# Two transformer layers on eight cores: order of the expert weight loads, and second k and v buffers in the WKV loop

## The reference

```python
x = x + _layernorm(_L0_attn_ref(_layernorm(x), ...))   # phase A: causal attention, 16 heads
x = x + _layernorm(_L0_ffn_ref(_layernorm(x), ...))    # phase B: attention, then a mixture of 8 experts
x = x + _layernorm(_L1_attn_ref(_layernorm(x), ...))   # phase C: the WKV recurrence
x = x + _layernorm(_L1_ffn_ref(_layernorm(x), ...))    # phase D: feed-forward with per-token LoRA
```

```python
for e in range(E):                       # E = 8, FFN = 2048, HID = 1024
    w1 = w13[e, :FFN]; w3 = w13[e, FFN:]
    g = silu(h @ w1.T) * (h @ w3.T)
    out = out + einsum('tf,hf->th', g, w2[e]) * wfull[:, e:e + 1]
```

```python
k = xk @ W_k.T; v = xv @ W_v.T; r = sigmoid(xr @ W_r.T)
new_p = max(p, u + k_t); so = exp(max(p - new_p, -30)); sc = exp(max(u + k_t - new_p, -30))
wkv_t = (so * q + sc * v_t) / (so + sc + 1e-9)
p, q = the same kind of update with the decay w
y = r * wkv;  out = y @ W_o.T
```

## Time and profile before

| | us |
|---|---|
| runs shown | 8763.72, 8841.24, 8338.84 |
| their median | 8763.72 |
| the profiled execution | 8342.41 |
| its span on core 3, the slowest core | 8340.7 |
| spans of the eight cores | 8273.8 to 8340.7 |
| PE busy on core 3 | 5667.9 (68%) |
| DVE busy | 2138.5 (26%) |
| ACT busy | 1978.9 (24%) |
| POOL busy | 170.9 (2%) |

### The profile page before, as it was taken

The page is one execution under the profiler, slowest core; times in us unless marked ns, Lnnn a source line. Parts: engine busy times, 40 slices in busy tenths (PEclk is TensorE's granted clock), DMA queues, the critical chain, the costliest instruction groups (busy, mean ns, idle before and its releaser), DMA issues.

```text
span 8340.7 us, 77939 instructions; the slowest of 8 cores (8273.8 to 8340.7 us)
## 1 busy us (share of the span) xinstructions
PE 5667.9 (68%) x21912; PEld 2164.4 (26%) x21912; DVE 2138.5 (26%) x3361; ACT 1978.9 (24%) x3520; POOL 170.9 (2%) x206
## 2 busy tenths in 40 slices
PE   5777764355887378889898989898821332537992
PEld 1222221021222133334343434343300111102330
DVE  3101112333111412222222222222237334230113
ACT  1256652214664110101010101001110232212111
POOL 0000000000000000000000000000000111000000
PEclk7656667665666689989899999999955666768995
DMA  2000002210000041332323231413120000221203
GB/s 61 11 1 1 1 12 61 60 21 1 1 1 11 1 82 34 68 61 51 59 54 61 41 71 31 81 33 69 36 84 23 12 12 18 62 61 26 56 2 79
DMA packets 82929, 313.97 MB, mean 38 GB/s; under 512 B 10136, under 2 KB 10520, under 8 KB 63032
## 3 DMA queue, kind: packets, MB, share of 16 engines
q0 software_dynamic: 26112, 207.99, 13.0%
q1 hardware_dynamic: 56416, 101.00, 4.5%
HBM read 483.31 MB, written 33.62 MB: 62 GB/s over the span
## 4 chain that ended last, share of the span: by engine, by line
PE 61%; DVE 12%; DMA 12%; ACT 8%; issue 6%; SPq 1%; POOL 1%; DVEq 0%; ACTq 0%; POOLq 0%
PE B_pso L1031 11%; PE B_psg L992 11%; PE B_psg L999 11%; DMA B_w3s<-b_w3T 3%; PE D_psi L1469 3%; PE D_pso L1487 3%; PE A_pmm L292 3%; PE A_pss L360 2%; PE C_pmm L1167 2%; PE B_pav L789 2%; PE A_pav L388 2%; ACT B_E L119 2%; ACT A_E L119 2%; PE B_pss L762 2%; DVE C_A L119 1%
## 5 line engine op out<-in xcount | busy, mean ns | idle before, releaser
L992 PE MATMUL B_psg<-B_H,B_w1s 128*128 128x512 bf16 x4096 | 980.7, 383 | 325.4 <-DMA B_w3s<-b_w3T 310.4
L999 PE MATMUL B_psg<-B_H,B_w3s 128*128 128x512 bf16 x4096 | 972.8, 381 | 0.0
L1031 PE MATMUL B_pso<-B_gall,B_w2b 128*128 128x512 bf16 x4096 | 902.9, 383 | 2.3 <-issue 0.5
L119 ACT ACTIVATE B_gsil<-B_psg 128x512 f32<-128x512 f32 x512 | 305.7, 597 | 2161.1 <-PE B_psg L992 2161.0
L119 DVE TENSOR_TENSOR B_gall<-B_gsil,B_psg 128x512 bf16<-128x512 f32 x512 | 351.9, 687 | 1759.0 <-PE B_psg L999 1759.0
L992 PEld LDWEIGHTS B_psg<-B_H,B_w1s 128*128 128x128 bf16 x4096 | 402.2, 98 | 819.8 <-issue 346.0
L1031 PEld LDWEIGHTS B_pso<-B_gall,B_w2b 128*128 128x128 bf16 x4096 | 401.7, 99 | 513.1 <-issue 45.1
L999 PEld LDWEIGHTS B_psg<-B_H,B_w3s 128*128 128x128 bf16 x4096 | 402.6, 98 | 489.5 <-issue 13.6
L1167 PE MATMUL C_pmm<-C_xk,C_wk 128*128 128x512 bf16 x256 | 72.7, 455 | 497.8 <-DVE C_Y L119 346.0
L119 ACT ACTIVATE B_E<-B_pss 128x512 bf16<-128x512 f32 (+3 forms) x640 | 341.2, 533 | 192.3 <-PE B_pss L762 135.2
L757 PE MATMUL B_pss<-B_qT,B_kT 32*128 32x512 bf16 (+3 forms) x640 | 284.4, 490 | 129.3 <-issue 108.2
(11 more groups left out here) (308 smaller groups left out, 4879.0 us busy)
## 6 DMA issues: line engine op xcount, KB each, us to landing
B_w1s<-b_w1T POOLq DMA_DIRECT2D x64, 1024.0 KB, 8.6
B_w3s<-b_w3T POOLq DMA_DIRECT2D x64, 1024.0 KB, 13.2
B_w2b<-b_w2T POOLq DMA_DIRECT2D x8, 4096.0 KB, 25.4
A_xc<-xin SPq DMA_DIRECT2D x32, 256.0 KB, 3.8
A_xr<-xin SPq DMA_DIRECT2D x32, 256.0 KB, 4.2
xm<-A_ost SPq DMA_DIRECT2D x32, 256.0 KB, 3.3
B_xc<-xm SPq DMA_DIRECT2D x32, 256.0 KB, 3.3
BT_xr<-xm SPq DMA_DIRECT2D x32, 256.0 KB, 3.2
```

The source lines that it names most:

```text
L119: instr = real(*a, **kw)
L992: mm = t.matmul(ps_g1[:], w1s[sb][:, dt * CH + fs * 128: dt * CH + (fs + 1) * 128], H[:, dt * T + c * CH:dt * T + (c + 1) * CH], start=(dt ...
L999: mm = t.matmul(ps_g3[:], w3s[sb][:, dt * CH + fs * 128: dt * CH + (fs + 1) * 128], H[:, dt * T + c * CH:dt * T + (c + 1) * CH], start=(dt ...
L1031: mm = t.matmul(ps_o[pb][:], w2b[:, ft * 1024 + ot * 128: ft * 1024 + (ot + 1) * 128], g_all[:, ft * 1024 + ch * CH: ft * 1024 + (ch + 1) ...
```

## The change

In phase B the tiles of the experts are allocated once for all experts, and the guards (`slab_guard`, `g1_free`, `evac` and the others) are no longer reset. In each expert the loads of slabs 0 and 1 are issued first, each pair guarded by the last matmul that read its buffer pair; the load of w2 is issued after them, guarded by `b_done` and by a new token `w2_users`, the last matmul that read `w2b`. In the loop over the slabs these first two pairs are taken from `pre_toks` and not loaded again in half 0.

In phase C `kb_` and `vb_` become two buffers each, used in turn. `A2` is no longer a tile; its contents are written over `pst`. The PSUM banks are freed by ACT's evacuations alone. Three tokens keep the order of the other tiles: `kv_consumed[idx]` (`y_tok` of two passes ago) ahead of the evacuations of k and v, `prev_y` ahead of those of r, and `prev_y` with `prev_ecv` ahead of Exp(k).

```diff
+        slab_guard = [None, None]
...
+        w2_users = None
+        bar9 = ctx.bar()
         for e in range(NEXP):
...
+                pre_toks = {}
+                for slab in range(2):
+                    sb = slab % 2
+                    pre_toks[(1, slab)] = load_wcast(
+                        ctx, W["w1T"][e * 128:(e + 1) * 128, slab * 4096:(slab + 1) * 4096],
+                        w1s[sb][:], f"qs1{sb}",
+                        pre=[slab_guard[sb]] + (bar9 if e == 0 else []))
+                    pre_toks[(3, slab)] = load_wcast(
...
                 w2tok = [load_wcast(ctx, W["w2T"][e * 128:(e + 1) * 128, :], w2b[:], "qw2B",
-                                    pre=[b_done] + (bar9 if e == 0 else []))]
-                slab_guard = [None, None]
...
+                                    pre=[b_done, w2_users] + (bar9 if e == 0 else []))]
...
+                        if (1, slab) in pre_toks:
+                            t1 = pre_toks.pop((1, slab))
+                            t3 = pre_toks.pop((3, slab))
+                        else:
...
                             b_done = pt
+                            w2_users = pt
...
-                kb_ = S3("C_kd", [128, T], F32)
-                vb_ = S3("C_vd", [128, T], F32)
+                kbufs = [S3("C_kd0", [128, T], F32), S3("C_kd1", [128, T], F32)]
+                vbufs = [S3("C_vd0", [128, T], F32), S3("C_vd1", [128, T], F32)]
...
-                            ctx.waits(s, [pt])
                             if dstb is not None:
+                                ctx.waits(s, [pt, kv_consumed[idx]])
...
                             else:
+                                ctx.waits(s, [pt, prev_y])
...
-                    ctx.waits(s, kv_tok)
+                    ctx.waits(s, kv_tok + [prev_y, prev_ecv])
...
+                    A2 = pst[:, 0:T]
...
-                    evac[0] = y_tok
-                    evac[1] = y_tok
+                    kv_consumed[idx] = y_tok
+                    prev_y = y_tok
```

More of the change, by code:

```diff
@@ L943, in phase_l0ffn @@
         esM.close()
+        esA = contextlib.ExitStack()
+        SA = lambda n, sh, dt: esA.enter_context(nc.sbuf_tensor(n, sh, dt))
+        PA = lambda n, sh: esA.enter_context(nc.psum_tensor(n, sh, F32))
+        g_all = SA("B_gall", [128, NTT * 1024], BF16)
+        w1s = [SA("B_w1s0", [128, NDT * CH], BF16), SA("B_w1s1", [128, NDT * CH], BF16)]
+        w3s = [SA("B_w3s0", [128, NDT * CH], BF16), SA("B_w3s1", [128, NDT * CH], BF16)]
+        _gs = SA("B_gsil0", [128, CH], F32)
+        gsil = [_gs, _gs]
+        w2b = SA("B_w2b", [128, NTT * 1024], BF16)
+        wf_row = SA("B_wfrow", [1, CH], F32)
+        wb_sb = SA("B_wb", [128, CH], F32)
+        ps_g1 = PA("B_psg1", [128, CH])
+        ps_g3 = PA("B_psg3", [128, CH])
+        ps_o = [PA("B_pso0", [128, CH]), PA("B_pso1", [128, CH])]
+        ps_wb = PA("B_pswb", [128, CH])
+        tmpo = gsil[0]
         wf_guard = [None]
@@ L947, in phase_l0ffn @@
         b_done = None
-        for e in range(NEXP):
[L949 to L965, removed]
-                w2tok = [load_wcast(ctx, W["w2T"][e * 128:(e + 1) * 128, :], w2b[:], "qw2B",
-                                    pre=[b_done] + (bar9 if e == 0 else []))]
-                slab_guard = [None, None]
[L970 to L974, removed]
@@ new lines, in phase_l0ffn @@
+        slab_guard = [None, None]
+        gs_tok = [None, None]
+        g1_free = None
+        g3_free = None
+        evac = {}
+        wb_free = None
+        w2_users = None
+        bar9 = ctx.bar()
+        for e in range(NEXP):
+            if True:
+                pre_toks = {}
[6 more added lines that the diff above has]
+                    pre_toks[(3, slab)] = load_wcast(
+                        ctx, W["w3T"][e * 128:(e + 1) * 128, slab * 4096:(slab + 1) * 4096],
+                        w3s[sb][:], f"qs3{sb}",
+                        pre=[slab_guard[sb]] + (bar9 if e == 0 else []))
+                w2tok = [load_wcast(ctx, W["w2T"][e * 128:(e + 1) * 128, :], w2b[:], "qw2B",
+                                    pre=[b_done, w2_users] + (bar9 if e == 0 else []))]
@@ L977, in phase_l0ffn @@
                         sb = slab % 2
[L978 to L985, removed]
+                        if (1, slab) in pre_toks:
+                            t1 = pre_toks.pop((1, slab))
+                            t3 = pre_toks.pop((3, slab))
+                        else:
+                            t1 = load_wcast(
+                                ctx, W["w1T"][e * 128:(e + 1) * 128, slab * 4096:(slab + 1) * 4096],
+                                w1s[sb][:], f"qs1{sb}", pre=[slab_guard[sb]])
+                            t3 = load_wcast(
+                                ctx, W["w3T"][e * 128:(e + 1) * 128, slab * 4096:(slab + 1) * 4096],
+                                w3s[sb][:], f"qs3{sb}", pre=[slab_guard[sb]])
                         for fs in range(4):
@@ L1045, in phase_l0ffn @@
         moe_tok = [radd]
+        esA.close()
         esH2.close()
@@ L1147, in phase_l1attn @@
                 A1 = S3("C_A1", [128, T], F32)
-                A2 = S3("C_A2", [128, T], F32)
                 rbuf = S3("C_rd", [128, T], BF16)
@@ L1152, in phase_l1attn @@
                 y_tok = None
+                prev_y = None
+                prev_ecv = None
+                kv_consumed = [None, None]
                 evac = {}
@@ L1155, in phase_l1attn @@
                 for dt in range(NDT):
+                    idx = dt % 2
+                    kb_ = kbufs[idx]
+                    vb_ = vbufs[idx]
                     wtok = []
@@ L1196, in phase_l1attn @@
                                            op0=ALU.add, op1=ALU.max)
-                    v.tensor_tensor(out=A2[:], in0=pst[:, 0:T], in1=A1[:], op=ALU.subtract)
-                    tv = v.tensor_scalar(out=A2[:], in0=A2[:], scalar1=-30.0, scalar2=None, op0=ALU.max)
+                    A2 = pst[:, 0:T]
+                    v.tensor_tensor(out=A2, in0=pst[:, 0:T], in1=A1[:], op=ALU.subtract)
+                    tv = v.tensor_scalar(out=A2, in0=A2, scalar1=-30.0, scalar2=None, op0=ALU.max)
                     ctx.waits(s, [tv])
-                    eo_tok = s.activation(out=A2[:], in_=A2[:], func=AF.Exp)
+                    eo_tok = s.activation(out=A2, in_=A2, func=AF.Exp)
                     v.scalar_tensor_tensor(out=ekv[:], in0=kb_[:], scalar=u_sc, in1=A1[:],
@@ L1207, in phase_l1attn @@
                     ctx.waits(v, [ec_tok, em_tok])
-                    tv = v.scalar_tensor_tensor(out=A2[:], in0=A2[:], scalar=EPS9, in1=ekv[:],
+                    tv = v.scalar_tensor_tensor(out=A2, in0=A2, scalar=EPS9, in1=ekv[:],
                                                 op0=ALU.add, op1=ALU.add)
@@ L1211, in phase_l1attn @@
                     ecv_tok = g.tensor_tensor(out=ekv[:], in0=ekv[:], in1=vb_[:], op=ALU.mult)
+                    prev_ecv = ecv_tok
                     ctx.waits(s, [tv])
-                    s.activation(out=A2[:], in_=A2[:], func=AF.Ln)
-                    rcp = s.activation(out=A2[:], in_=A2[:], func=AF.Exp, scale=-1.0)
+                    s.activation(out=A2, in_=A2, func=AF.Ln)
+                    rcp = s.activation(out=A2, in_=A2, func=AF.Exp, scale=-1.0)
                     ctx.waits(v, [rcp])
@@ L1218, in phase_l1attn @@
                     v.tensor_tensor(out=A1[:], in0=A1[:], in1=ekv[:], op=ALU.add)
-                    v.tensor_tensor(out=A1[:], in0=A1[:], in1=A2[:], op=ALU.mult)
+                    v.tensor_tensor(out=A1[:], in0=A1[:], in1=A2, op=ALU.mult)
                     y_tok = v.tensor_tensor(out=Ybf[:, dt * T:(dt + 1) * T], in0=A1[:],
                                             in1=rbuf[:], op=ALU.mult)
-                    evac[0] = y_tok
-                    evac[1] = y_tok
+                    kv_consumed[idx] = y_tok
+                    prev_y = y_tok
                 y_last = [y_tok]
```

## The result

| | before | changed |
|---|---|---|
| median of ten runs, us | 8786.10 | 8341.92 |
| lowest and highest, us | 8323.21, 8956.81 | 8006.47, 8544.54 |
| ratio, with its 95% interval | | 0.9619 (0.9590 to 0.9648) |
| the profiled execution, us | 8342.41 | 8006.47 |
| span of core 2 | 8316.5 | 8004.8 |

The changed kernel is 3.8% faster. The medians lie well above the profiled executions because in many executions of either kernel the cores of one die, or of both, show a lower mean granted clock (0.73 on cores 4 to 7 against 0.78 on cores 0 to 3 in the changed kernel's 8544.54 us), and the ratio leaves those executions out.

The account below looks back on a forecast made before the run. PE was taken to bound the experts except for waits on w3; phase C was held by its serial chain. Gains of 251.9 + 15.4 + 26.5 + 23 = 317 us gave 8026 us, range 7990 to 8460 us.

Parts of the forecast that it names:

- the 317 us: Whole kernel, core 3: summed gain of 251.9 + 15.4 + 26.5 + 23 us, taken off the profiled execution.
- 8447 us: Whole kernel: time after if read from a run like the median one, 8763.7 - 317 us.
- the waits at the start of experts 1 to 7: Up projection, core 3: of 265.2 us waiting for w3, 13.3 us stay for the residual add; gain 251.9 us.
- the warm-up: First 16 matmuls after each of 7 waits: 2.2 us less each, 15.4 us in all.
- expert 0: First expert's start: first slab no longer behind w2, so PE starts earlier; gain 26.5 us on core 3.
- The estimate of 7 us to landing: Expert 0's first two slabs, by the skill page's rule: some 7 us, gaining about 6 us more; not used in the sum.
- what is late next: Experts: w2 lands within 29.2 us, wanted 110 us later; slab 2 lands at 3361, wanted at 3375.
- The cover of 14 us: Slab 2 of each expert: lands 14 us before PE wants it; without it each microsecond counts 8 times.
- phase C: Weight loads behind POOL's second product hold PE; each pass gains 3.3 us, 7 passes 23 us.
- The clock: Rival, experts: without rests the chip grants less clock and the gain is lost, 8528 us; chance 0.05.
- The rule of the Trainium skill: Experts, within the clock rival: 13/16 of the clock makes 2650 us into 3262, time about 8640 us.
- The wider overlap in phase C: Rival: if loads did not stand behind POOL's product, 105 us gained instead of 23, 7944 us; chance 0.04.

Follow-up runs that it names:

- run of the experts alone: The changed kernel with phase C put back as it was before the change; ratio to the kernel before 0.9639 (0.9597 to 0.9681).
- the order alone changed: The changed kernel with an expert's first four slab loads also waiting for the end of the expert before; ratio to the kernel before 0.9759 (0.9685 to 0.9832).

## Why the prediction was right and wrong

**Wrong: the time that the forecast named.** The step is "I forecast 8026 us, 3.8% below the profiled execution": the 317 us were taken from the profiled execution, 8342.41 us. The percentage is what was measured (0.9619), and the changed kernel's profiled execution took 8006.47 us. But the time before is given as a median, 8763.72 us in the runs shown, and against that 8026 us claims 8.4%. Ten runs of each kernel have medians of 8786.10 and 8341.92 us, 316 us above my number. I had seen the 421 us between median and profile, and worked out 8447 us for it, but let it only widen the range, without a chance of its own among the cases. With two of three runs shown at 8764 and 8841 us, that reading was the more likely one for a median. What should have been forecast is the ratio of like with like, and a time on the level on which the time before is told.

The 8447 us would also have been high by 105 us: the medians fell by 444 us, not 317. Why is open, but such a median moves by itself. The kernel before has 8686.19 and 8754.94 us in the two series of the experiments, and the run with single k and v buffers, whose ratio is 0.9613, has a median of 8012.83 us where the changed kernel has 8341.92.

**Partly luck: how near 8006 is to 8026.** On core 2 the stretches that the change touches gave 282.8 us of the 292.8 forecast, and 29 us that nobody forecast came from the rest.

**Right: the waits at the start of experts 1 to 7.** 251.9 us were to go and 13.3 us to stay. The wait for w3 is gone there, 15 waits of 1.9 us stay, and the experts' stretch lost 264.3 us on core 2 and 292.0 us on core 3, against 269.8 and 293.8. The run of the experts alone gives 0.9639.

**Right: the warm-up.** The first 16 matmuls of expert 1 take 3.45 us.

**Right within its bounds: expert 0.** PE waits 20.1 us on core 2 and 16.1 us on core 3, where 18.7 were forecast for both; the gains are 20.7 and 29.1 us, against 22.1 and 26.5. The estimate of 7 us to landing, which the prediction works out for the two slabs from the page DMA: Bandwidth & Descriptors of the Trainium skill (Anatomy of one DMA), is not what the trace shows: the w3 that PE waits for on core 2 lands 14.1 us after its issue, and the median of all is 12.3 us.

**Right: what is late next.** w2 and slab 2 do not show up: the down projection waits for no load, and w3 is waited for once. The cover of 14 us was shown by using it up, though by queued bytes rather than by POOL's time.

**Right in mechanism, a little high: phase C.** 23 us were forecast and 18.5 came. The term that was mis-sized is the gain of a pass, 3.3 us: the wait shrank by 3.0 us, and the whole pass by 2.6 us. That the weights behind POOL's product are the new wait is shown by moving them.

**The rivals.** The clock did not give the gain back: the windows of the experts show 0.98 to 1.00 in the profiled execution on all eight cores, and the medians, which leave no execution out, fell by more than the forecast. But the rival was not empty, as the 140 us at 0.82 in the run of the experts alone show. The rule of the Trainium skill that was weighed there (TensorE: Matmul & The Clock Gate, Seeing it yourself) sets 13/16, or 0.81, for a whole die. In the profiled executions of the kernel before and the changed one the experts do not show it. In the run of the experts alone its level appears, though on two cores of a die and not on the other two.

The wider overlap in phase C, put at 105 us in place of 23, was rightly tied to the loads' place in the queue. With that moved, 67 + 18.5 = 86 us came.

## What to carry to other kernels

When loads share a queue, put first what is wanted first: with a 4 MB tile wanted 110 us later standing ahead of the 1 MB tiles wanted at once, 57% of the gain in the experts was the order, and the rest was fetching earlier. When a wait is removed, look at what stands ahead in the queue of whatever comes second: here it was three small loads behind a 4.5 us product on POOL, and a second set of buffers bought nothing until the queues let two passes overlap. When the time before is a median and the trace is of an execution 421 us below it, forecast the ratio, and take the time after from the median.

## What the runs showed that was not expected

A load waits for the bytes ahead of it in its queue and not only for its issue: with a second 4096 KB load just ahead, w3 of a slab took 38.7 us from issue to landing instead of 12.7, at the same moment of issue relative to PE. Whether a load in another queue would wait as well was not tried.

The second surprise is how little of ACT's added work shows: 8 evacuations per pass, put between two activations of a serial chain, left a wait of 5.23 us there and cost the chain nothing.

The third is in the traces of all nine kernels, over all their cores. In each of the pairs 0 and 1, 2 and 3, 4 and 5, 6 and 7, the core that issues its first expert load later waits longer for w3. In the changed kernel core 3 issues at 2884.7 us and waits 16.1 us, core 2 at 2903.2 us and waits 20.1 us; with the order alone changed core 1 waits 120.6 us in all and core 0 146.2. So the size of such a wait depends on the core that is read. What the two cores of a pair share is not shown.
